# Sorted order of a mixture-of-experts stage from one-hot products, token rows gathered instead of scattered

## The reference

```python
h = _layernorm(x, axis=-1) * (1 + cb) + sb           # "h2" in the kernel
probs = softmax(h @ gate_w.T)                        # 8 experts
top_p, top_i = top_k(probs, 2)
y = sum over the two: top_p * ((silu(h @ fc1[e].T) * (h @ fc2[e].T)) @ proj[e].T)   # width 176
shared = silu(h @ shared_fc1.T) * (h @ shared_fc2.T) @ shared_proj.T                # width 704
y = y + sigmoid(h @ shared_gate_w.T) * shared
x = x + gb * y                                       # gb is one row per batch
```

## Time and profile before

| | |
|---|---|
| Three runs, median (lowest to highest) | 441.76 us (441.0 to 442.19) |
| The profiled execution's own time | 442.69 us |
| Its span, first to last instruction | 441.0 us |
| Granted TensorE clock, mean | 0.962 |
| TensorE matmul busy | 385.2 us (87%) |
| VectorE busy | 235.3 us (53%) |
| ScalarE busy | 143.7 us (33%) |
| GpSimd busy | 145.6 us (33%) |

### The profile page before, as it was taken

How to read it: one execution, slowest core, us unless ns; L and a number is a source line. 1 busy time by engine, 2 the same in 40 slices (tenths; PEclk the granted TensorE clock), 3 DMA queues, 4 the chain that set the end, 5 groups by cost and what they waited for, 6 DMA issues and landing times.

```text
span 441.0 us, 9797 instructions
## 1 busy us (share of the span) xinstructions
PE 385.2 (87%) x3833; PEld 232.8 (53%) x3834; DVE 235.3 (53%) x543; ACT 143.7 (33%) x296; POOL 145.6 (33%) x251
## 2 busy tenths in 40 slices
PE   3985989999899998986998998718999999999784
PEld 3344465574557556435644644503466666666353
DVE  3166666896689579213554731003255655655367
ACT  2565608434662503530213111001243333342000
POOL 8304103400610340010000077753037666667400
PEclk9999799999999999998999999956999999999898
DMA  8999400000000000590000023232023333321196
GB/s 263 294 292 256 142 3 3 1 4 4 1 1 4 1 1 5 173 288 30 0 0 1 1 98 110 100 113 70 25 74 117 102 107 91 112 70 50 33 338 231
DMA packets 32573, 39.83 MB, mean 90 GB/s; under 512 B 4231, under 2 KB 29202, under 8 KB 32532
## 3 DMA queue, kind: packets, MB, share of 16 engines
q1 hardware_dynamic: 29124, 30.74, 24.3%
q0 software_dynamic: 3408, 8.51, 5.5%
HBM read 23.24 MB, written 16.91 MB: 91 GB/s over the span
## 4 chain that ended last, share of the span: by engine, by line
PE 65%; DVE 10%; ACT 6%; another core or an unknown queue 6%; issue 5%; DMA 4%; SPq 1%; POOL 0%; DVEq 0%; POOLq 0%; ACTq 0%
PE work L1341 12%; PE at_ps L1686 11%; PE work L1370 5%; PE work L1351 4%; PE work L1707 4%; PE at_ps L1406 3%; PE work L1498 3%; PE work L1709 3%; PE work L1548 2%; PE at_ps L1370 2%; DMA arena<-ys_tokens 2%; PE at_ps L1670 2%; PE o_even L1461 1%; PE at_ps L1548 1%
## 5 line engine op out<-in xcount | busy, mean ns | idle before, releaser
L1351 PE MATMUL work<-sdn_sb,hs 128*128 128x256 f32 x192 | 49.3, 398 | 13.0 <-issue 8.8
L621 POOL DMA_INDIRECT ys_tokens<-er_pos,goal_u x39 | 40.9, 1049 | 45.1 <-DVE er_pos L1264 37.8
L592 POOL DMA_INDIRECT xs_sorted<-h2tok,pos_u x32 | 31.6, 989 | 72.6 <-DVE pos_u L955 63.2
L1686 PE MATMUL at_ps<-arena 128*128 x156 | 54.5, 472 | 0.4 <-ACT arena L847 0.4
L1027 DVE TENSOR_TENSOR hs<-work,hs 128x512 f32<-128x512 f32 (+1 forms) x24 | 16.6, 691 | 61.4 <-PE work L1341 47.6
L1351 PEld LDWEIGHTS work<-sdn_sb,hs 128*128 128x128 f32 x192 | 34.2, 190 | 27.9 <-issue 17.9
L641 ACT ACTIVATE hs<-work 128x512 f32<-128x512 f32 (+1 forms) x24 | 14.3, 596 | 99.8 <-PE work L1341 82.8
L555 POOL TENSOR_TENSOR sq<-sq,sg 128x512 f32<-128x512 f32 x8 | 10.0, 1274 | 99.1 <-issue 99.1
L1341 PE MATMUL work<-h2T,sup_sb 128*128 128x512 f32 x80 | 36.2, 599 | 0.7 <-ACT hs L641 0.4
L1686 PEld LDWEIGHTS at_ps<-arena 128*128 128x128 f32 x156 | 26.5, 190 | 14.9 <-issue 6.6
L851 ACT ACTIVATE arena<-at_ps 128x176 f32<-128x176 f32 x39 | 12.4, 318 | 57.7 <-PE at_ps L1686 43.0
(11 more groups left out here) (241 smaller groups left out, 752.2 us busy)
## 6 DMA issues: line engine op xcount, KB each, us to landing
xs_sorted<-arena SPq DMA_DIRECT2D x10, 526.0 KB, 11.9
h2tok<-xs_sorted SPq DMA_DIRECT2D x20, 263.0 KB
arena<-ys_tokens SPq DMA_DIRECT2D x8, 512.0 KB, 7.4
arena<-in_e_up SPq DMA_DIRECT2D x8, 352.0 KB, 5.7
x_sb<-in_x SPq DMA_DIRECT2D x4, 512.0 KB, 7.0
out_rows<-x_sb SPq DMA_DIRECT2D x16, 128.0 KB, 4.8
sup_sb<-in_s_up SPq DMA_DIRECT2D x2, 640.0 KB, 4.9
hs<-in_wmod SPq DMA_DIRECT2D x1, 1024.0 KB, 7.8
```

Of the source, the lines that this page charges most:

```text
L592: g.indirect_dma_start(out=xs_dram, out_offset=bass.IndirectOffsetOnAxis(ap=pos_u[:, k, t:t + 1], axis=0), in_=h2tok[:, t, :], in_offset=N ...
L621: g.indirect_dma_start(out=ys_dram, out_offset=bass.IndirectOffsetOnAxis(ap=goal_u[:, i:i + 1], axis=0), in_=yout[:, q % 2, u, :], in_offs ...
L1351: ins = t_.matmul(o[:, t * HID:(t + 1) * HID], hs[0:m, f, tk], sdn_sb[0:m, f, :], start=(f == 0), stop=(f == FTS - 1))
L1686: ins = t_.matmul(at_ps[2 + u % 2][:, 0:2 * FE], xT[:, u % 2, k * P:(k + 1) * P], eup[:, bass.ds(e, 1), k, :].rearrange("p a n -> p (a n)" ...
```

## The change

The zero fill of `xs_dram`, the 32 scatters, the seven extra columns and the loads of sorted rows go. Instead h2 is stored to `h2_dram` in token order, by SP, one block at a time. VectorE makes, for each choice k and tile t of tokens, a one-hot matrix of each token's row within its tile of the sorted order (`row_columns`: 128 x 128) and, for its sorted tile, columns with token number and weight (`tile_columns`: 2 x 40). TensorE sums the 32 products of the two in one PSUM bank: the result says for each row of each sorted tile which token and weight stand there, zero where none does. `read_records` turns that into `token_u`, `goal_u`, `rec` and `in_batch1`, all at once for all tiles. GpSimd gathers the rows of each tile from `h2_dram` by indirect DMAs into the same slots `xt`: four pairs at once, two more as slots come free, then one pair after each `put_rows`. `goals` goes.

The shared parts: five stand at the new place "places" (the second down part of block 1 and four up parts of block 2; VectorE's new steps are threaded between them), four at "gather" (the rest of block 2), after the products. `EARLY_UP` is 0: all eight parts of the last block stand behind the experts, and `combine` is threaded between its up parts on VectorE. VectorE's middle groups are unrolled, since `rec` and `in_batch1` are indexed by tile. The one-hot matrices take the space of `h2tok`, the tile columns that of `h2T` and of the q, k and v weights, which become one tile. `iota_f` has 128 columns instead of 40.

```diff
-XS_ROWS = ESLOTS * P
-HX = HID + 7
 NOWHERE = 1 << 20
-X_TOK, X_W0, X_BATCH, X_TURN, X_DW, X_NONE, X_EXP = range(HID, HX)
+NREC = 2
+RCHUNK = 8
...
-EARLY_UP = 4
+EARLY_UP = 0
 SHARED_PARTS += [("U", NBLK - 1, f) for f in range(EARLY_UP)]
 FILL_PLACES = [(4, "gates", 1), (4, "half", 1), (4, "second", 1), (4, "norm", 4), (4, "stats", 2), (4, "ln", 3),
-               (4, "transposed", 2), (4, "top2", 1), (4, "scatter", len(SHARED_PARTS))]
+               (4, "transposed", 2), (4, "top2", 1), (4, "places", 5), (4, "gather", 4)]
...
+        wqkv = sb("wqkv_sb", [P, 3, KC, HID])
+        wq_sb, wk_sb, wv_sb = (wqkv[:, i, :, :] for i in range(3))
+        wgate_sb, wo_sb = (sb(n, [P, KC, HID]) for n in ("wgate_sb", "wo_sb"))
+
+
+        in_row = h2tok[:, :, :].rearrange("p t c -> p (t c)").rearrange("p (k t r) -> p k t r", k=TOPK, t=NTILE)
+        in_tile = [b[:, 0:NTILE * NREC * ESLOTS].rearrange("p (t a i) -> p t a i", t=NTILE, a=NREC)
+                   for b in (h2T[:, :, :, :].rearrange("p a k n -> p (a k n)"), wqkv[:, :, :, :].rearrange("p w k n -> p (w k n)"))]
...
-            sp.wait_ge(zero_ready, 6)
-            for i in range(ESLOTS // 4):
-                sp.dma_start(xs_dram[i * BLK:(i + 1) * BLK, :].rearrange("(t p) c -> p t c", p=P),
-                             atm_zero).then_inc(xs_zero, 16)
...
+            def store_h2(b):
+                sp.wait_ge(h2tok_ready, b + 1)
+                sp.dma_start(h2_dram[b * BLK:(b + 1) * BLK, :].rearrange("(t p) c -> p t c", p=P),
+                             h2tok[:, b * TPB:(b + 1) * TPB, :]).then_inc(h2_stored, 16)
+
+            for b in range(NBLK - 1):
+                store_h2(b)
...
-            sp.wait_ge(xs_ready, 16 * TOPK * NTILE)
-
-            def load_pair(q, slot):
-
-                sp.dma_start(xt[:, slot, :, :],
-                             xs_dram[bass.ds(q * (2 * P), 2 * P), :].rearrange("(t p) c -> p t c", p=P)
-                             ).then_inc(ld_xt[slot], 16)
-
-            for q in range(XPAIRS):
-                load_pair(q, q)
-            with sp.Fori(0, ESLOTS // EGRP - 1) as grp:
-                for u in range(XPAIRS):
-                    sp.wait_ge(xt_full, grp * EGRP + 2 * u + 2)
-                    sp.wait_ge(goal_ready, grp * EGRP + 2 * u + 2)
-                    load_pair(grp * XPAIRS + u + XPAIRS, u)
+            store_h2(NBLK - 1)
...
-            pool.wait_ge(xs_zero, 16 * (ESLOTS // 4))
-            pool.wait_ge(posu_ready, 1)
-            pool.wait_ge(h2tok_ready, NBLK)
-            for k in range(TOPK):
-                for t in range(NTILE):
-                    g.indirect_dma_start(out=xs_dram, out_offset=bass.IndirectOffsetOnAxis(ap=pos_u[:, k, t:t + 1], axis=0),
-                                         in_=h2tok[:, t, :], in_offset=None).then_inc(xs_ready, 16)
...
-            def goals(q):
+
+            def gather_pair(q):
 
                 slot = q % XPAIRS
-                pool.wait_ge(ld_xt[slot], 16 * (q // XPAIRS + 1))
-                if q >= XPAIRS:
-                    pool.wait_ge(y_out, 2 * (q - XPAIRS) + 2)
-                for u in range(2):
-                    steps.did(g.tensor_scalar(second[:, slot, u:u + 1], xt[:, slot, u, X_EXP:X_EXP + 1],
-                                              texp1[:, 2 * q + u:2 * q + u + 1], None, ALU.is_equal))
-                steps.sync()
-                steps.did(g.tensor_tensor(turned[:, slot, :, :], xt[:, slot, :, X_TURN:X_NONE + 1],
-                                          second[:, slot, :].unsqueeze(2).broadcast_to([P, 2, 3]), ALU.mult))
-                steps.sync()
-                g.tensor_tensor(goal[:, slot, :, :], turned[:, slot, :, :], xt[:, slot, :, X_TOK:X_BATCH + 1],
-                                ALU.add).then_inc(goal_ready, 2)
-                pool.wait_ge(goal_ready, 2 * q + 2)
-                steps.did(g.tensor_scalar(goal_u[:, 2 * q:2 * q + 2], goal[:, slot, :, 0], float(NOWHERE), None, ALU.add))
-                steps.sync()
+                for u in range(min(2, ETILES - 2 * q)):
+                    i = 2 * q + u
+                    if q >= XPAIRS:
+                        pool.wait_ge(xt_full, i - EGRP + 1)
+                    g.indirect_dma_start(out=xt[:, slot, u, :], out_offset=None, in_=h2_dram[:, :],
+                                         in_offset=bass.IndirectOffsetOnAxis(ap=token_u[:, i:i + 1], axis=0)
+                                         ).then_inc(ld_xt[slot], 16)
...
-            goals(0)
-            goals(1)
+            pool.wait_ge(h2_stored, 16 * NBLK)
+            pool.wait_ge(rec_full, 1)
+            pool.wait_ge(token_ready, 1)
+            for q in range(XPAIRS):
+                gather_pair(q)
+            pool.wait_ge(goal_ready, 1)
+            ahead = XPAIRS + 2
+            for q in range(XPAIRS, ahead):
+                gather_pair(q)
             for q in range(EPAIRS):
-                if q + 2 < EPAIRS:
-                    goals(q + 2)
                 put_rows(q)
+                if q + ahead < EPAIRS:
+                    gather_pair(q + ahead)
...
-            v.tensor_copy(pos_u[:, :, :], pos[:, :, :]).then_inc(posu_ready, 1)
+            steps.did(v.tensor_scalar(tile_i[:, :, :], pos[:, :, :], 0.0, None, ALU.add))
+            steps.sync()
+            steps.did(v.tensor_scalar(tile_i[:, :, :], tile_i[:, :, :], 7, None, ALU.arith_shift_right))
+            steps.sync()
+            steps.did(v.tensor_copy(tile_f[:, :, :], tile_i[:, :, :]))
+            steps.sync()
+            steps.did(v.scalar_tensor_tensor(out=row_f[:, :, :], in0=tile_f[:, :, :], scalar=-float(P), in1=pos[:, :, :],
+                                             op0=ALU.mult, op1=ALU.add))
+            steps.sync()
+
+        def tile_columns(dve, v, steps, k):
+
+            def spread(ap):
+                return ap.unsqueeze(2).broadcast_to([P, NTILE, ESLOTS])
+
+            token, weight = in_tile[k][:, :, 0, :], in_tile[k][:, :, 1, :]
+            steps.did(v.tensor_tensor(weight, iota_f[:, 0:ESLOTS].unsqueeze(1).broadcast_to([P, NTILE, ESLOTS]),
+                                      spread(tile_f[:, k, :]), ALU.is_equal))
+            steps.sync()
+            steps.did(v.tensor_tensor(token, weight, spread(tok_f[:, k, :]), ALU.mult))
+            steps.sync()
+            v.tensor_tensor(weight, weight, spread(pw[:, :, k]), ALU.mult).then_inc(rec_made, 1)
+
+        def row_columns(dve, v, k):
+
+            for t in range(0, NTILE, RCHUNK):
+                if k == 0 and t == 0:
+                    dve.wait_ge(h2_stored, 16 * NBLK)
+                v.tensor_tensor(in_row[:, k, t:t + RCHUNK, :], iota_f[:, :].unsqueeze(1).broadcast_to([P, RCHUNK, P]),
+                                row_f[:, k, t:t + RCHUNK].unsqueeze(2).broadcast_to([P, RCHUNK, P]), ALU.is_equal
+                                ).then_inc(rec_made, 1)
+
+        def read_records(dve, v, steps):
+
+            dve.wait_ge(rec_full, 1)
+            v.tensor_copy(rec[:, :, :], at_ps[3][:, 0:NREC * ESLOTS].rearrange("p (a i) -> p a i", a=NREC)).then_inc(rec_ready, 1)
+            dve.wait_ge(rec_ready, 1)
+            steps.did(v.tensor_scalar(turn_at[:, :], rec[:, 0, :], float(TOK) + 0.5, float(TOK), ALU.is_ge, ALU.mult))
+            steps.sync()
+            steps.did(v.tensor_tensor(token_1[:, :], rec[:, 0, :], turn_at[:, :], ALU.subtract))
+            steps.sync()
+            steps.did(v.tensor_scalar(token_0[:, :], token_1[:, :], 1.0, None, ALU.max))
+            steps.sync()
+            v.tensor_scalar(token_u[:, :], token_0[:, :], -1.0, None, ALU.add).then_inc(token_ready, 1)
+            steps.did(v.tensor_scalar(empty[:, :], rec[:, 0, :], 0.5, float(NOWHERE), ALU.is_lt, ALU.mult))
+            steps.did(v.tensor_scalar(in_batch1[:, :], token_1[:, :], float(SEQ) + 0.5, None, ALU.is_ge))
+            steps.sync()
+            steps.did(v.tensor_tensor(goal[:, :], rec[:, 0, :], empty[:, :], ALU.add))
+            steps.sync()
+            v.tensor_scalar(goal_u[:, :], goal[:, :], -1.0, None, ALU.add).then_inc(goal_ready, 1)
...
-                        dve.wait_ge(xs_zero, 16 * (ESLOTS // 4))
...
+            parts = FILL[NBLK, "places"]
+            for n, (kind, blk, i) in enumerate(parts):
+                if n < 2:
+                    tile_columns(dve, v, steps, n)
+                (mult_up if kind == "U" else add_down)(blk, i)
+                if 1 <= n <= TOPK:
+                    row_columns(dve, v, n - 1)
+            read_records(dve, v, steps)
+            fill(NBLK, "gather")
...
-                if not isinstance(i, int) or i:
+                if i:
                     dve.wait_ge(y_out, i)
-                dve.wait_ge(goal_ready, i + 2)
                 for t in range(2):
-                    v.scalar_tensor_tensor(out=row_gain[:, t, :], in0=row_step, scalar=goal[:, (u // 2) % XPAIRS, t, 2:3],
+                    v.scalar_tensor_tensor(out=row_gain[:, t, :], in0=row_step, scalar=in_batch1[:, i + t:i + t + 1],
...
```

(16 more changed lines are left out.)

75 lines of the change are left out of this document (33 added, 42 removed).

## The result

The changed kernel took 458.15 us (median of 4 runs, 454.57 to 461.3), the kernel before 441.38 us on the same chip (439.54 to 442.19); the ratio is 1.0385 with a 95% interval from 1.0337 to 1.0433. The profiled run took 454.57 us, its span is 452.8 us: 11.9 us more than the span of before. The forecast was 434.4 us with 427 to 441, faster. Both the time and the sign were wrong.

What follows compares the result with a forecast made beforehand. It took TensorE as the bound, with holes near 39.6 us and around the scatter. The terms, from -4.0 at the head to +1.7 of low clock, sum to -7.4, so 441.8 - 7.4 = 434.4 us, range 427 to 441.

Steps and rivals of the forecast that it cites:

- Head, -4.0: Near 39.6 us: without the ten zero stores TensorE's code block comes in time and its 3.98 us gap goes.
- Slow issue, -13.2: TensorE's down products of block 2 beside the scatters: their slow issue, tied to the long scatter train, goes, 13.2 us.
- +3.9: Routing on VectorE: its new steps make TensorE wait for PSUM banks, 3.9 us, bounds 2 and 8.
- +7.0: Records on TensorE: 32 fp32 products as 64 instructions add 7.0 us, all on the path.
- +0.8: Start of the experts: TensorE loads expert registers behind a wait for VectorE, no longer under matmuls, 0.8 us.
- the four parts -16.8: Four shared parts of the last block that stood before the experts go from there, saving 16.8 us.
- Expert stage, +1.0: Expert stage: GpSimd's added gathers make it fall behind; about 1 us reaches TensorE, bounds 0 to 6.
- rival B: Slow issue not from the scatter train, or the shorter train has it too: 450.6 us, slower, chance 0.10.
- Rival A: GpSimd becomes the bound of the expert stage if gathers are slow: 448.7 us at 1.8 us each, chance 0.13.
- Tail, 13.8 - 1.6 = +12.2: Behind the experts: four more shared parts cost 13.8 us; last sums waiting less for VectorE save 1.6.
- low-clock spell of +1.7: New waits leave TensorE sparse enough for one more spell at low clock, 1.7 us, bounds 0 to 3.4.
- The chance of 0.15 for slower: Chance given to the changed kernel being slower, against 0.80 for faster and 0.05 for the same.

Runs made afterwards that it cites:

- r1_before: The kernel before, unchanged, run again on a chip with the slow issue beside the scatters: 443.74 us.
- f2_after: The changed kernel, unchanged, on a chip without the slow issue: 437.95 us, ratio 1.0279 to the kernel before.
- r6_before: The kernel before, unchanged, run once more for its trace on a chip without the slow issue: 425.59 us.
- r4_breaks: The kernel before, with GpSimd waiting for all landings after every fourth of the 32 scatters, on a chip with the slow issue: 441.51 us, ratio 0.9957.
- e2_sp_rows: The changed kernel without gathers, SP loading as many bytes of consecutive rows by plain DMAs: 439.04 us, ratio 0.9932 to the kernel before.
- f1_two_breaks: The kernel before, with a wait for all landings after the 11th and 22nd scatter only, on a chip without the slow issue: 428.61 us, ratio 1.0062.

## Why the prediction was wrong, point by point

- Head, -4.0: the mechanism was right, the size wrong. The gap of 3.98 is in the other traces of kernels with the zero stores too, 3.98 in `r1_before` and 2.88 to 3.43 in seven more, and in none of the changed kernel's. The reading as late code fits the traces. The first 16 KB packet of the instruction queue runs inside the gap in all nine (from 40.44 to 41.83 us in the kernel before, where TensorE stands from 39.60 to 43.58), and in the eleven traces without the stores it starts at 36.4 to 37.4 us; for which engine it is, they don't tell. But without the gap TensorE soon waits for VectorE, and little stays:

```profile
45.12 0.67 PE L1444 MATMUL at_ps<-arena 32*64 32x128 f32 x24 [1.87 <-DVE gate_pair L1114]
```

  The first of the four gate products of block 1, 2 and 3, f2_after against r6_before, where the spells of low clock behind 100 us are alike: 40.94 against 44.91 (-4.0), 80.42 against 83.00 (-2.6), 121.97 against 123.99 (-2.0). On P even that was lost: the router's transpose of block 3 comes at 240.07 against 239.42. Two spells at half clock came in that the kernel before didn't have, and why isn't shown:

```profile
86.70:90.10 3.40, 3.40 (x47) 1.54 (x50) 2.15 (x4) 2.44 (x5) 0.00 (x0) 0.50 0.00 0
117.40:120.80 3.40, 3.40 (x54) 2.33 (x57) 0.52 (x1) 0.00 (x0) 1.05 (x2) 0.50 0.00 0
```

  The Trainium skill's sentence that the cost of crossing a block of instructions is mostly hidden (Runtime: NRT & Kernel Launch, "Instruction fetch mechanics") would have given 0 here, and 0 to 2 is what stayed; yet the gap itself is real, so it was the cover behind it that made the page's number come out.
- Slow issue, -13.2: right on P (48 products in 12.00 us), and the train of indirect DMAs has to do with it as guessed: `r4_breaks` breaks it up and the slow issue goes. What was missing is that it isn't on every chip: on R, T and U there was nothing to gain.
- The chain between, +3.9, +7.0, +0.8 and the four parts -16.8: the waits came as 1.37 and 1.98, the 64 record products took 7.1 us, and the start has a gap of 1.98 instead of the 0.8. From the down products at 240.35 to the experts it is 58.06 us against 76.42, -18.4, where the terms give -18.3.
- Expert stage, +1.0: this is the step that failed, +18.8 on P. GpSimd's own figures were right (5.35 us per pair), and over the 14 pairs that have both its pace costs next to nothing: with the same work for GpSimd `f2_after` has a stage of 99.51 us, in which VectorE waits 1.7 us for landings, `e2_sp_rows` without any gather 99.33. The failure is in rival B's argument, "the expert stage has two per pair and none of it". That was a row of the kernel before, with pauses of over 2 us between pairs. The change makes it four per pair, 5.35 us against 4.83, so that GpSimd hardly pauses: my own sum had computed that lag, and I didn't see that it is a train without end. In its place the runs showed TensorE's signals held up on P, Q and S, 10.7 us of idle TensorE and a low clock behind it. Rival A looked at GpSimd's pace and rival B at the hold-up, in the right place only A. Their 448.7 and 450.6 us were nearer than the forecast by luck, for neither had the mechanism at its place: A's cost is close to nothing here, and B's 16.2 us did go.
- Tail, 13.8 - 1.6 = +12.2 and a low-clock spell of +1.7: +12.7 on U against T, both with one spell of 6.8 us. On P +10.7: the spell that the kernel before has at 414.62 fell away there (40 matmuls in 17.43 us) instead of being added.
- Clock: the spells in the expert stage cost 7 us where the sum had 1.7 in all. Some 1.7 of them are the spell at its start, which `f2_after` has too (294.87 to 298.28); the other 5 stand behind the waits that the hold-up makes.
- The range took its bounds from one chip. On U the 437.95 us lie in it, which is luck, and the change is still 2.8% slower, because the kernel before is too. The chance of 0.15 for slower left out what I couldn't have put a number to but could have named: a gain of 13.2 us resting on an effect of which no row gave the cause.

## What to carry to other kernels

Before you give GpSimd more indirect DMAs, add up what it issues per step against the length of the step: where its pauses vanish, TensorE's signals can be held up for microseconds on some chips (0.4 to 7.4 us here), and neither GpSimd's pace nor the bytes show it. Where waits end with "remote" or "issue" although the producer's row ended earlier, look at what GpSimd issues just then. A large gain that rests on a stall without a named cause should be checked on more than one chip, and if the kernel then makes more of what went with the stall, the same stall is a rival with its own price.

The pauses are worth little as a remedy so far: `r4_breaks` is level with the kernel before on S (0.9957, interval across 1), and `f1_two_breaks` 0.6% slower on U. If trains of 14 us are short enough, two pauses on a chip of the first kind should start the experts near 302 us, as on T and U, instead of 316; that wasn't run there, and no version was found that beats the kernel before on both kinds.

## What the runs showed of the hardware that I had not expected

- Signals of TensorE alone come late, by 0.4 to 7.4 us in the expert stages and by 19.4 us beside the scatters (280.11 to 299.48 in `r1_before`), in two forms: as rises held back and let go together 0.05 us apart, and as TensorE's own issue at one matmul per 2 to 3 us. The unbroken train at the first late signal was 8.3 us in the expert stage (P, Q and S alike) but over 19 us beside the scatters, where the signals up to 271.67 came on time, and the 10.0 us of the eight gathers brought none. What sets that, and what in the chip holds them, no run tells.
- Chips differ in it: P, Q and S have it in every trace in which the scatters or four DMAs per pair run unbroken, R, T and U in none, with trains up to 101 us. No chip is known to have been used twice, so that a chip keeps its kind isn't shown. The kernel before takes 441 to 443 us on the one kind and 425 to 427 on the other, and nearly all of that is one place in its trace.
- The kinds differ in a second thing: records of rises are missing in every trace of P, Q and S, also where nothing is held up (of some 314 rises of TensorE 3 to 31, of some 545 of VectorE 20 to 45, of 258 of ScalarE 14 to 32), and at most 2 per engine in those of R, T and U. Every time on record comes with a recorded span and clock. Whether the recording itself has a part in the hold-up is a rival that no run tests.
- TensorE stops for 2.88 to 3.98 us near 40 us in each of nine traces with ten stores of 526 KB under way, and in none of eleven without them; that a block of code comes late there is the likely reading, not a tested one.
